# Attention with a three-pass split of fp32: one head's spreading product behind the last transposes of P, and a new order of VectorE's and ScalarE's work in the last two slots

## The reference

```python
def _L0_attn_ref(x, w_qkv, b_qkv, w_o, b_o):
    qkv = x @ w_qkv.T + b_qkv
    q, k, v = jnp.split(qkv, 3, axis=-1)
    ...
    scores = jnp.einsum('bhfc,bhtc->bhft', k, q)
    causal = jnp.triu(jnp.ones((s, s), dtype=bool))
    scores = jnp.where(causal[None, None], scores, MASKED_BIAS)
    attn = jax.nn.softmax(scores, axis=-2)
    vals = jnp.einsum('bhft,bhfc->bhtc', attn, v)
    vals = vals.transpose(0, 2, 1, 3).reshape(b, s, PART)
    return vals @ w_o.T + b_o
...
x = x + _layernorm(_L0_attn_ref(_layernorm(x)))
x = x + _layernorm(_L0_ffn_ref(_layernorm(x)))
```

## Time and profile before

| | us |
|---|---|
| median of 3 runs | 1556.33 |
| lowest and highest | 1554.25, 1561.55 |
| the profiled execution | 1556.48 |
| its span, first to last instruction | 1554.6 |
| around the span | 1.9 |
| busy in the span: TensorE matmuls / VectorE / ScalarE / GpSimd | 1490.1 / 980.1 / 699.1 / 624.3 |

### The profile page before, as it was taken

How to read it: one execution, slowest core, us unless ns; L and a number is a source line. 1 busy time by engine, 2 the same in 40 slices (tenths; PEclk the granted TensorE clock), 3 DMA queues, 4 the chain that set the end, 5 groups by cost and what they waited for, 6 DMA issues and landing times. The chain is left out here.

```text
span 1554.6 us, 24973 instructions
## 1 busy us (share of the span) xinstructions
PE 1490.1 (96%) x8032; PEld 1312.7 (84%) x8032; DVE 980.1 (63%) x2105; ACT 699.1 (45%) x1499; POOL 624.3 (40%) x1162
## 2 busy tenths in 40 slices
PE   7999999999999999999999679999999999999996
PEld 5888888888888888888887569999999999999996
DVE  7475575664765755756645656666666666666663
ACT  5364464573664655645636533333333333333331
POOL 2252362453443624614522534444444444334433
PEclk9999999999999999999999779999999999999998
DMA  6212112112112131121201612222212121111111
GB/s 230 82 38 73 56 29 89 34 51 64 50 43 72 37 92 33 40 78 35 52 21 38 237 58 69 68 67 67 67 67 67 67 67 64 59 60 59 61 62 41
DMA packets 46926, 102.92 MB, mean 66 GB/s; under 512 B 5040, under 2 KB 21424, under 8 KB 46896
## 3 DMA queue, kind: packets, MB, share of 16 engines
q1 hardware_dynamic: 46896, 102.54, 21.3%
HBM read 60.06 MB, written 25.69 MB: 55 GB/s over the span
## 5 line engine op out<-in xcount | busy, mean ns | idle before, releaser
L1529 PE MATMUL ps_f<-wagh,x2Th 128*128 128x364 f32 x768 | 256.7, 334 | 4.4 <-DVE f L1391 2.9
L1529 PE MATMUL ps_f<-wagl,x2Th 128*128 128x364 f32 x768 | 253.8, 331 | 0.0
L1529 PE MATMUL ps_f<-wagh,x2Tl 128*128 128x364 f32 x768 | 253.5, 330 | 0.0
L963 PE MATMUL ps_o<-xTh,wh 128*128 128x512 f32 x504 | 207.6, 412 | 2.9 <-DVE xTl L562 2.9
L963 PE MATMUL ps_o<-xTh,wl 128*128 128x512 f32 x504 | 198.6, 394 | 0.0
L963 PE MATMUL ps_o<-xTl,wh 128*128 128x512 f32 x504 | 197.7, 392 | 0.0
L1529 PEld LDWEIGHTS ps_f<-wagh,x2Th 128*128 128x128 f32 x768 | 145.7, 190 | 7.2 <-issue 5.0
L1529 PEld LDWEIGHTS ps_f<-wagl,x2Th 128*128 128x128 f32 x768 | 145.8, 190 | 1.3
L1529 PEld LDWEIGHTS ps_f<-wagh,x2Tl 128*128 128x128 f32 x768 | 145.6, 190 | 0.0
L580 DVE TENSOR_TENSOR PTl<-ps_t,PTh 128x512 fp32r<-128x512 f32 (+1 forms) x192 | 111.1, 599 | 46.7 <-ACT PTh L767 43.2
L1262 POOL TENSOR_TENSOR var_eps<-mv,eps 128x1 f32<-128x1 f32 x95 | 19.0, 200 | 302.3 <-DVE mv L1325 302.3
(11 more groups left out here) (175 smaller groups left out, 3577.0 us busy)
## 6 DMA issues: line engine op xcount, KB each, us to landing
kst<-kst SPq DMA_DIRECT2D x64, 256.0 KB, 3.6
xt<-in_x SPq DMA_DIRECT2D x32, 512.0 KB, 4.0
out<-outs SPq DMA_DIRECT2D x32, 512.0 KB, 3.0
xs<-in_x SPq DMA_DIRECT2D x24, 512.0 KB, 4.6
valsT<-vt SPq DMA_DIRECT2D x64, 128.0 KB, 2.3
vraw<-valsT SPq DMA_DIRECT2D x32, 256.0 KB, 4.2
raw<-in_wqkvT SPq DMA_DIRECT2D x12, 512.0 KB, 6.5
wag_raw<-in_wagT SPq DMA_DIRECT2D x8, 546.0 KB, 5.3
```

The lines of the kernel that those rows point to most:

```text
L963: done = pe.matmul(ps[:, :], w[:, k, c:c + P], xT[:, k, :], start=(k == 0 and w is wh and xT is xTh), stop=(k == KD - 1 and w is wl), skip ...
L1529: last = pe.matmul(ps_f[:, g, 0:GW], a[:, k, :], w[:, k, cols], start=(k == 0 and a is x2Th and w is wagh), stop=False, skip_group_check=True)
```

## The change

Three things, all but one inside the loop's body only:

1. TensorE, slot 6: the spreading product of head 5 goes behind the scores of head 7 and the two transposes of the third group of head 5.
2. VectorE, slots 6 and 7: the reciprocal goes to the front. In slot 7 the order becomes reciprocal, first and second remainder of P, sum of values, third remainder, q0's remainder (before: first remainder, sum, second remainder, reciprocal, q0's remainder, third remainder).
3. ScalarE, slot 7: the copies of the first two groups of P go ahead of the copy of the values' lower half.

In the last body slot 7 loses its special order on VectorE: the sum of values comes ahead of both remainders.

```diff
--- before.py
+++ after.py
@@ -679,26 +679,34 @@
                         x_back(1, 1, b + 1)
                     if last and h == 9:
                         first_attention_out()
-                    if h in (X_SLOT, X_SLOT + 2):
+                    if h in (BARE, BARE + 1) and not last:
+                        reciprocal(h, b)
+                    if h == X_SLOT:
                         p_lo(h - 1, 0, b)
                         vals_sum(h - 2, b)
                         p_lo(h - 1, 1, b)
+                    elif h == BARE + 1 and not last:
+                        p_lo(h - 1, 0, b)
+                        p_lo(h - 1, 1, b)
+                        vals_sum(h - 2, b)
                     else:
                         if h >= 2:
                             vals_sum(h - 2, b)
                         if 1 <= h <= NH:
                             for g in range(2):
                                 p_lo(h - 1, g, b)
-                    if h < NH:
+                    if h < (NH if last else BARE):
                         reciprocal(h, b)
                     if h == BARE and not last:
 
                         p_lo(h - 1, 2, b)
                         scores_max(h + 1, b)
+                    if h == BARE + 1 and not last:
+                        p_lo(h - 1, 2, b)
                     if h not in SOON:
                         lows(h, 0, b, last)
                     lows(h, 1, b, last)
-                    if 1 <= h <= NH and (h != BARE or last):
+                    if 1 <= h <= NH and (h not in (BARE, BARE + 1) or last):
                         p_lo(h - 1, 2, b)
                     if h == X_SLOT and not last:
                         x_low(1, b + 1)
@@ -840,11 +848,13 @@
                         exps(h, b)
                     if h in SOON:
                         highs(h, 0, b, last)
-                    if h >= 2:
+                    if h >= 2 and (h != BARE + 1 or last):
                         vals_lo_part(h - 2, b)
                     if 1 <= h <= NH:
                         for g in range(2):
                             p_hi(h - 1, g, b, h - 1 == BACKWARD and not last)
+                    if h == BARE + 1 and not last:
+                        vals_lo_part(h - 2, b)
                     if h == X_SLOT and not last:
                         x_high(1, b + 1)
                     if h != 3:
@@ -1105,8 +1115,6 @@
                         transpose_p(h - 1, 1, b, h - 1 == BACKWARD and not last)
                     turns(h, 1, b, last)
                     steps(h, 1, b, last)
-                    if h == BARE and not last:
-                        masked_weights(h - 1, b, True)
                     turns(h, 2, b, last)
                     if last and h == 8:
                         first_output(0)
@@ -1114,6 +1122,8 @@
                         scores(h + 1, b, last)
                     if 1 <= h <= NH:
                         transpose_p(h - 1, 2, b)
+                    if h == BARE and not last:
+                        masked_weights(h - 1, b, True)
 
             pe.wait_ge(consts, 14)
             for t in range(NT):
```

## The result

| | before | after |
|---|---|---|
| median of the runs shown with the result, us | 1557.12 (4 runs) | 1542.20 (4 runs) |
| lowest and highest | 1554.25, 1561.55 | 1540.47, 1543.97 |
| ratio of the two, 95% interval | | 0.9902 (0.9875 to 0.9928) |
| the profiled execution, its span | 1556.48, 1554.6 | 1543.97, 1542.1 |
| one loop pass (mean of the fourth to the sixth) | 106.27 | 104.43 |

The change is faster by 14.9 us of median (11.2 to 19.5 by the interval). Between the two profiled executions lie 12.5 us. The length of a pass is the distance between the starts of SyncE's x loads, one per pass; the three agree within 0.1 us. Seven passes give 7 x 1.84 = 12.9 us. What stands behind the loop, the last body and the output phase, took 764.4 us before and 764.8 after (from the last such load on, less one pass), and the loop's first load starts at 42.5 us in both.

The account below looks back on a forecast made before the run. TensorE, busy 1490.1 of 1554.6 us, was taken as the bound, so only its gaps could be won. Seven passes of 1.36 us (9.5) plus 2.9 for part 3 made 12.4 us, giving 1544.0, range 1541 to 1547.

Parts of the forecast that it names:

- Part 1: TensorE, slot 6: product behind scores and transposes starts q0's second half 1.41 us earlier; a 0.4 us wait stays.
- Part 2: VectorE, slot 6: head 6's reciprocal first delays sum and remainders by 0.05 us and wins nothing alone.
- Part 3: Slot 7's new order: the value product's wait for the last remainder goes, 0.45 us in five passes, 2.9 in all.
- the ring: Chain through head 7's softmax to slot 7's first remainder and head 6's transposes: 0.6 us of slack.
- Contention: GpSimd's work of heads 6 and 7 beside VectorE's remainders and sums: costed at nothing.
- The last body: Transposes about 0.5 us later, swallowed by a following 3.24 us wait for GpSimd: cost 0.
- B: Rival, slot 6: reciprocal delays the release, or a small wait appears in slots 7 to 9; 0.5 us per pass, 1547.5; chance 0.12.
- C: Rival, slot 6: GpSimd and VectorE block each other, part 1's gain falls to 0.1 us, 1552.5; chance 0.05.
- D: Rival: the chain through head 7's softmax stretches and delays TensorE's transposes, 0.6 us a pass, 1560.5; chance 0.03.

Follow-up runs that it names:

- the lengthened chain: The changed kernel with two more unused 128x512 reductions on VectorE ahead of the first remainder in slot 7: 1544.20 us, a pass of 104.97.
- the order alone: The changed kernel with the spreading product put back ahead of the scores, leaving the new VectorE and ScalarE orders: 1551.24 us, ratio 0.9960.
- the product inside q0: The changed kernel with the spreading product three matmuls later, behind the first step of q0's second half: 1538.33 us, ratio 0.9888.
- slot 6 reordered: The changed kernel with slot 6 ordered as slot 7, both remainders ahead of the sum and ScalarE's copy of values later: 1539.43 us, ratio 0.9890.
- the last kernel: The kernel before with two moves only, the product inside q0's second half and q0's remainder behind P's third: 1537.62 us, ratio 0.9881.

## Why the prediction was right

It gave 1544.0 us and a pass of 104.5; measured were 1542.2 and 104.43. The passes hold 12.9 us of gain against the 12.4 forecast, so the mechanism is what was forecast; the other 2 us of the median are in no step of the prediction (see "Still open"). By its steps:

**Part 1** gave 1.41 us a pass, 1.36 with the reciprocal's delay. Up to q0's first matmul 1.33 were measured, and the 0.10 us behind it in q0's half I had not counted: the pass comes out a little better than forecast by that, not by anything foreseen. The move alone shortened a pass by 1.50. The release was read rightly: the product starts 2.12 us behind k0's last matmul, 2.04 before. The remaining wait was called 0.3 to 0.4 us in the profile and is shown as 0.16. What I had worked out was the distance from start to start, 0.4, and that is right (0.45 from transposes to product beyond the 0.14 of the kernel without wait); my error was to expect it as the number in brackets.

**Part 2**, the reciprocal at the front of slot 6: 0.05 us of delay taken, 0.04 measured (11.9 against 11.6 us in seven waits); from k0's last matmul to the product it is 2.12 us in the changed kernel and 2.07 with the move alone, again 0.05. "This wins nothing alone" holds too, for slot 7's reciprocal as well.

**Part 3** gave 0.45 us in five passes and less in two, 2.9 in all; it is 0.41 to 0.46 in each of the seven passes, 3.0 in all. The cause named, q0's remainder ahead of the last one of P, is shown by the kernel with that step alone. What the prediction missed is that the move by itself already frees a part of it: from this product to the transposes it was 2.30 us before, 2.16 with the move alone, 1.87 with the change. So of the 2.9 us put down to part 3, the new order is worth 7 x 0.34 = 2.4 behind the move, and the move the rest. The slack of the ring was 0.6 us in the prediction and 0.67 by the lengthened chain.

**Contention** cost nothing, as taken: 2.07, 0.83, 0.74 and 1.29 us side by side. The sum reads PSUM, one SBUF tensor and a scalar per partition, and it held nobody: GpSimd's weight, which starts 0.05 us behind it, took its 0.20 us, the diagonal its 0.83. So the scalar did not act as a second SBUF input here. Beside the product of two SBUF tensors the same weight took 0.29. The Trainium skill, page "SBUF — State Buffer", section "SBUF: two separate sides", has VectorE lock the shared port pair when an instruction has two SBUF inputs. The trace agrees in which instructions meet; how long a lock held it does not show, since the weight and the product overlap for 0.24 us (333.21 to 333.45) and only 0.09 were lost.

**The last body** cost nothing that shows: 764.4 and 764.8 us from the loop's end to the program's, where the profiles of all kernels here lie between 762.4 and 765.5. As forecast, the transposes' longer wait is taken off the wait for GpSimd (0.36 and 0.41 us).

**The rivals.** B: the release slipped by 0.08 us, not 0.5; with the move alone it slipped by 0.03. C: nothing is stretched. D: the transposes of slot 7 do not wait, with 0.77 us to spare by the rows, and the chain through head 7's softmax is no longer than its parts were before.

**Still open** are some 1.4 to 3.3 us. Every kernel run in several rounds gains more by its median than by its passes: the change 14.9 and 15.5 us against 12.9 and 13.0, the move alone 13.2 against 10.5, the order alone 5.7 against 2.4, the product inside q0 18.6 against 15.9, slot 6 reordered 17.5 against 16.1, the last kernel 18.9 against 15.6. The last kernel's 18.9 is also more than the 16.6 us that the prediction gave as the most; its passes stay within it. These are not seven independent findings, as several kernels share the runs of the kernel before, and for the change the interval (11.2 to 19.5 us) takes in the 12.9. The four kernels run once give no clear sign (13.1 against 13.2, 11.3 and 11.6 against 9.1, 9.4 against 11.0 us). The profiled executions of before and after don't hold the surplus (12.5 us). Among profiled executions two stretches outside the loop differ. What stands behind the loop took 764.8 and 763.9 us in two executions of the changed kernel. The other is the program's start. The busy table from 20 to 45 us, in the profile after:

```profile
20.00:45.00 25.00, 25.00 (x105) 20.55 (x104) 15.97 (x17) 13.47 (x16) 0.00 (x0) 0.91 0.62 198
```

and in the changed kernel run again:

```profile
20.00:45.00 25.00, 25.00 (x110) 20.73 (x109) 17.18 (x20) 12.72 (x16) 0.00 (x0) 0.96 0.68 218
```

The granted clock is 0.91 in the one (and before) and 0.96 in the other, whose loop begins at 40.5 us instead of 42.5. Both are executions of the same changed kernel, so these 2 us are not its work. The mean granted clock of a whole span was 0.981 to 0.985 in the kernel before and 0.983 to 0.986 in the others, and 0.001 of 1555 us is 1.6 us. So the surplus may lie in the clock; that is not shown, and whether shorter waits in the loop raise it was not tried.

## What to carry to other kernels

When an engine waits, look first for work of its own behind the waiting instruction that needs none of what is late: here ten matmuls moved ahead (eight of the scores, two transposes) took 1.3 of 1.8 us, three of 512 columns more took the rest, and no other engine had to change for it. Of a bundle of reordered steps often one carries the gain; run each alone, and leave out the ones that only put an instruction ahead of the late chain. Read the length of a loop pass beside the median: here it resolved 0.1 us where the runs of one kernel scattered by 2 to 7, and it added up over the parts.

## What the runs showed that I had not expected

- A wait of TensorE is shown far below its cost, or not at all. 0.16 us in brackets was 0.46 a pass; 0.29 us lost in slot 8 with the move alone had no row in the list of waits. Start to start against a place without a wait shows both.
- The 512-column matmul behind 128-column transposes held its successor off for 0.31 us, behind a 384-column product for 0.23. What stands ahead of a long run was worth 0.1 us of it.
- VectorE's product of two SBUF tensors (0.40 us) made the one GpSimd instruction beside it 0.09 us longer; the later ones kept their durations.
